# Two 3x3 convolutions that rotate through three pairs of PSUM banks for four, the two parts of a pair three taps apart for four

## The reference

```python
x = x + _L0_conv_ref(_gn(x), w_real, w_imag, b_real, b_imag)  # FFT, complex 3x3 convolution, inverse FFT
x = x + _L1_conv_ref(_gn(x))                                  # rows gated by the sign of a dot product
x = x + _L2_conv_ref(_gn(x), L2_conv_W)                       # 3x3 convolution, 16 to 16 channels
x = x + _L3_conv_ref(_gn(x), L3_conv_weight)                  # 3x3 convolution, 16 to 16 channels
```

## Time and profile before

| | us |
|---|---|
| median of 3 runs | 5523.62 (5523.53 to 5527.76) |
| the profiled execution, its own time | 5522.16 |
| its span, first to last instruction | 5520.4 |
| PE busy | 4636.8 (84%) |
| DVE busy | 3411.5 (62%) |
| ACT busy | 2593.9 (47%) |
| mean granted TensorE clock | 0.926 |

### The profile page before, as it was taken

How to read it: one execution, slowest core, us unless ns; L and a number is a source line. 1 busy time by engine, 2 the same in 40 slices (tenths; PEclk the granted TensorE clock), 3 DMA queues, 4 the chain that set the end, 5 groups by cost and what they waited for, 6 DMA issues and landing times. The chain is left out here.

```text
span 5520.4 us, 227169 instructions
## 1 busy us (share of the span) xinstructions
PE 4636.8 (84%) x84352; PEld 2919.4 (53%) x84352; DVE 3411.5 (62%) x10276; ACT 2593.9 (47%) x7377; POOL 956.5 (17%) x718
## 2 busy tenths in 40 slices
PE   3798699968999598995989959899599986988678
PEld 0455455545656365563655636566365644555455
DVE  0587816877178761887528874387835878168770
ACT  4355345553455434553445534456345553444434
POOL 0123101240022300223002230022201231012400
PEclk9999899988999799997999979999799998999889
DMA  5343024420344104441144401443024430232104
GB/s 167 101 123 95 3 86 133 122 75 3 114 125 125 52 11 126 124 125 33 34 122 123 126 15 45 133 125 114 2 62 140 123 92 3 88 96 68 37 3 125
DMA packets 294829, 471.65 MB, mean 85 GB/s; under 512 B 22288, under 2 KB 97104, under 8 KB 294224
## 3 DMA queue, kind: packets, MB, share of 16 engines
q1 hardware_dynamic: 294224, 462.41, 27.9%
HBM read 328.10 MB, written 134.22 MB: 84 GB/s over the span
## 5 line engine op out<-in xcount | busy, mean ns | idle before, releaser
L1123 PE MATMUL ps<-x,conv_s 32*32 32x512 f32 x49104 | 1816.1, 603 | 41.3 <-ACT shared L565 20.7
L1123 PEld LDWEIGHTS ps<-x,conv_s 32*32 32x32 f32 x49104 | 1253.6, 104 | 576.0 <-issue 338.5
L432 POOL TENSOR_TENSOR acc<-acc,x 128x512 f32<-128x512 f32 x512 | 669.0, 1307 | 4222.4 <-ACT x L494 4222.4
L1050 PE MATMUL ps<-hil,shared 128*128 128x256 f32 x4096 | 993.6, 386 | 0.0
L494 ACT ACTIVATE x<-ps,vec 128x256 f32 (+1 forms) x1024 | 490.1, 495 | 1002.8 <-PE ps L1050 1002.8
L1050 PEld LDWEIGHTS ps<-hil,shared 128*128 128x128 f32 x4096 | 740.4, 190 | 273.8 <-issue 194.1
L738 DVE SCALAR_TENSOR_TENSOR shared<-xin,trig 128x256 f32<-128x256 f32 x2048 | 811.7, 436 | 60.3
L565 ACT ACTIVATE shared<-ps,vec 64x512 f32<-64x512 f32 (+1 forms) x768 | 525.0, 684 | 574.4 <-PE ps L1123 564.8
L734 DVE TENSOR_SCALAR xin<-xin,vec 128x512 f32<-128x512 f32 x512 | 367.2, 717 | 626.9 <-DMA out<-shared 495.9
L1035 PE MATMUL ps<-shared 32*32 32x512 f32 x16384 | 669.3, 613 | 0.0
L554 ACT ACTIVATE x<-ps,vec 128x512 f32 x512 | 347.2, 684 | 471.5 <-PE ps L1123 471.5
(11 more groups left out here) (147 smaller groups left out, 3671.1 us busy)
## 6 DMA issues: line engine op xcount, KB each, us to landing
shared<-x SPq DMA_DIRECT2D x512, 256.0 KB
xin<-x SPq DMA_DIRECT2D x512, 256.0 KB
out<-shared SPq DMA_DIRECT2D x512, 256.0 KB
shared<-t_strip SPq DMA_DIRECT2D x576, 96.0 KB, 3.4
hil<-t_hil SPq DMA_DIRECT2D x1, 560.0 KB, 3.3
trig<-t_trig SPq DMA_DIRECT2D x1, 512.0 KB, 4.1
x<-t_bias SPq DMA_DIRECT2D x1, 512.0 KB, 5.1
x<-w_mix SPq DMA_DIRECT2D x1, 288.0 KB, 3.2
```

The lines of the kernel that those rows point to most:

```text
L432: nc.gpsimd.tensor_tensor(acc, acc, strip_of(s), ALU.add).then_inc(y_added, 1)
L1050: mm = pe.matmul(split_in(ps[:, BY + 2 * odd + e, :])[:, int(q < 2), :], xt[:, e, q, :], hil[:, q, 0:HALF], start=False, stop=True, skip_g ...
L1123: mm = pe.matmul(ps[TM * cg:TM * cg + TM, banks[k], :], conv_s[TM * rg:TM * rg + TM, kw, second, :], x1[TM * rg:TM * rg + TM, of, kw:kw + ...
```

## The change

`DEPTH` goes from 4 to 3 and `LAG` from `TAPS + 1` to `TAPS`. The places of the banks are now (0,1), (2,3), (4,5) in both convolutions; banks 6 and 7 are no longer used by pairs. The output slots of `evict3` keep their rotation of four pairs, under a name of its own. ACT's register loops are gone: all evictions of an image are written out. The wait for `v_bias3` on PE is gone.

```diff
-DEPTH = 4
-LAG = TAPS + 1
+DEPTH = 3
+SLOT_PAIRS = 4
+LAG = TAPS
@@ ACT
-                with act.Fori(0, PAIRS // DEPTH) as j:
-                    for e in range(DEPTH):
-                        evict2(j * DEPTH + e, banks2(e))
+                for n in range(PAIRS):
+                    evict2(n, banks2(n))
                 root(i, 4, ZV)
                 act.wait_ge(v_bias3, i + 1)
-                with act.Fori(0, PREPARING[0] // DEPTH) as j:
-                    for e in range(DEPTH):
-                        evict3(j * DEPTH + e, banks2(e), e, j)
-                for n in range(PREPARING[0], PREPARING[1] + 2):
-                    evict3(n, banks3(n), n % DEPTH, n // DEPTH)
+                for n in range(PAIRS):
+                    evict3(n, banks3(n), n % SLOT_PAIRS, n // SLOT_PAIRS)
                     if more and n == PREPARING[0] + 1:
                         root(i + 1, 0, 0)
                         root(i + 1, 1, ZV, ZR)
-                with act.Fori((PREPARING[1] + 2) // DEPTH, PAIRS // DEPTH) as j:
-                    for e in range(DEPTH):
-                        evict3(j * DEPTH + e, banks2(e), e, j)
@@ PE, first3
                     if kw == 0:
-                        if n == DEPTH - 1:
-                            pe.wait_ge(v_bias3, i + 1)
-                            due()
                         before = [k for k in range(n) if banks3(k) == banks3(n)]
```

## The result

| | before | after |
|---|---|---|
| median of 5 runs, us | 5524.2 (5523.53 to 5527.76) | 5553.69 (5545.6 to 5563.97) |
| profiled execution's own time | 5522.16 | 5553.69 |
| its span | 5520.4 | 5551.9 |
| mean granted TensorE clock | 0.926 | 0.926 |

The ratio is 1.0054, 95% interval 1.0039 to 1.0069: slower by 0.5%, 29 us, where +18 was forecast.

The account below looks back on a forecast made before the run. PE was taken to bound the convolutions. Terms -16.4 - 2.1 + 26.6 + 2 + 3 + 5 = +18.1 us on 5522.16 gave 5540.3; 5541.5 was predicted, own range 5534 to 5554, eight in ten 5524 to 5580.

Parts of the forecast that it names:

- What bounds, and the rates: Convolutions: bound by PE, 32.1 ns a record with both parts in a slot; a one-part slot costs nearly as much.
- The case with a drop after each of eight gaps: Pair 8: the clock falls after every new gap, 13.6 us for 2 in the sum, 5553 us; chance 0.07.
- The sign of being wrong, pairs over 3.1 us: Rolling loops: pairs taking longer than 3.1 us, with PE idle behind evictions or between parts, would refute the prediction.
- The wait at pair 8: conv3: pair 8 waits for pair 7's eviction, shifting all behind it by 3.32 us an image, +26.6 us.
- Rival 2: Pairs 8 to 13 don't follow pair 8's shift; faster, -18.5 us if none arrives, 5505 us; chance 0.12.
- The clock: PE's gap of some 2.3 us ahead of pair 8 may lower the granted clock: +2 us, bounds 0 to 13.6.
- The lag: Three rolling loops an image: one more full slot, two fewer single ones, -0.69 us each, -16.4 us in all.
- The thin waits: Less slack for evictions in rolling loops, +3 us, and for `halved` between a pair's two parts, +5 us.
- Rival 3: Thin margins cost 0.1 us at 464 pairs or 0.3 at 160 evictions, +46 to +48 us, 5588; chance 0.14.
- The forecast's loop: conv3's rolling loops, eviction to eviction: 9.05 us for three pairs against 9.24 today, so no longer.
- ACT written out: conv2's end: the last activation starts 0.26 us sooner once an image, -2.1 us; elsewhere only slack.
- All eight banks: The skill's rule implies a cost everywhere; the forecast expected bank shortage at pair 8 only, not in rolling loops.

Follow-up runs that it names:

- The wait alone: Kernel before, with only one wait more: pair 8 of conv3 waits for pair 7's eviction; ratio 1.0062.
- the swapped order: Places 2 and 1 for 1 and 2 in pairs 8 to 13: changed kernel 0.9947; kernel before 0.9965; four places, lag 3, ACT written out 0.9943.
- narrow stores: Only 64 of each strip's 512 output columns stored: kernel before 5451.1 us, lag 3 alone 5451.7, changed kernel 5476.3.
- filling: Changed kernel with 32 more records of matmuls per image ahead of pair 8's wait; ratio 1.0023.

## Why the prediction was right, and where not

**The number.** 5541.5 us were predicted and 5553.69 measured, inside the range and at the upper edge of the forecast's own (5534 to 5554). That it came so near is in part luck: in the ledger a term that was left out and one that was too small, +13.0 and +4.8 us, make up the difference, against 4 in the other direction. The case with a drop after each of eight gaps names 5553 us, but there were five drops, not eight, and the rest is the stalls.

**What bounds, and the rates.** Right: conv2's rate did not move, 32.1 ns a record. The sign of being wrong, pairs over 3.1 us, was badly set for conv3: the 3.08 us a pair came from conv2, and conv3's pairs 14 to 31 have a median spacing of 3.17 us in both kernels.

**The wait at pair 8.** Right in place, mechanism and size: 3.32 us forecast, 3.3 measured in the images without a drop (43.6 for 40.3), in all eight; the whole block shifted behind it. The wait alone and the swapped order show it from both sides. Rival 2 (the next stage doesn't follow) is out.

**The clock.** The mechanism was right, the term mis-sized: 2 us forecast, 6.8 measured at the two places, inside the bounds of 0 to 13.6. I took "most gaps leave no drop" from pair 14's eight gaps with one drop (two of the eight are in the earlier trace rows). The other profiles show that such a gap of 2.3 us is followed by a drop in none to seven of eight images, with the order around it hardly changed. One kernel's profile was no measure of the odds; the middle of the bounds would have been right here, and nothing found tells the odds ahead.

**The lag.** The structure gave what was summed, about: the remainder of the ledger, -14.6, lies between the forecast's -10.5 and -18.5. That is no proof of the lag's -16.4: with narrow stores the lag alone gave back 8 to 10 us, its drops taken off. What was left out of the sum is the stalls, +13 us in the profile. I had their row and charged them to ACT's code alone, as a bound of 10; written out alone that code makes 38.9 us of them for 36.1. The full stores make them. That the shorter lag makes them longer is only likely: the four kernels with full stores, lag 3 and no filling have 43 to 50 us, the four with lag 4 and four places 36 to 41, but lag 5 didn't lower them, and it is one profile each. Why the same stores hold PE longer there stays open. That what PE waits for is its instructions was argued, not shown: the profile says only that its weight loads wait for issue.

**The thin waits.** 8 us forecast; at most 4 in the ledger, 3 in the profiles with narrow stores. With three places and lag 4 conv3's pairs drew apart to 3.55 us, with lag 3 they don't. Rival 3, in which every pair pays, is out. The forecast's loop had the right sign but was 0.6 us short where it binds. PE's weight loads do wait longer for issue (446.8 us for 338.5), but not by the third place alone: with the lag alone it is 396.8, with pair 8's wait alone 389.5.

**ACT written out.** 0.26 us an image forecast, 0.32 found; too small for the runs. That the addresses are what takes the time fits another row: conv3's evictions, in register loops too before but at constant addresses, started 0.04 us after the last matmul there already (median).

**All eight banks.** The Trainium skill (Perfetto Trace Analysis, Matmul Optimizations) asks for the use of all eight PSUM banks. Here three places in the swapped order (0.9947) and four (0.9943) can't be told apart: what costs is not a bank left unused but a pair that takes the banks of the pair just completed. The fourth place is worth something with lag 4: three places cost 1.4% there, of which the wait at pair 8 alone is 0.6. The Trainium skill's other page cited (TensorE: Matmul & The Clock Gate, A second HAM failure mode: psum-queue depth-cycling) bears on it as forecast with little weight: idle gaps between groups did let the clock fall, in five images at 1.7 us. No bank's wait did so in the rolling loops; there the clock fell once, and twice before, behind stalls of 2 us. The forecast saw none of it before, since the earlier trace rows show conv2 alone; these are in conv3.

## What to carry to other kernels

When a rotation of buffers gets shorter, don't only check the steady loop: list for every point where the rotation is broken (a block with its own order) which buffer comes next and how long ago it was released. One reuse of a buffer just filled, eight times in 5.5 ms, cost more than the shorter lag's whole gain; permuting two places gave it back, and a wait that had stood at pair 14 all along. A gap of a few us on TensorE carries a risk of 1.7 us for the clock on top, and one profile doesn't tell how often it strikes.

## What the runs showed of the hardware

- After gaps of 2.3 us, alike in length and with nearly the same work on both sides, the granted clock fell from 2.4 to 1.2 GHz in 0 to 7 of 8 images, depending on the kernel; each fall lasted about 3.4 us and cost 1.7. Where matmuls cut the gap to 1.21 us, it stayed up in all eight.
- PE waits for no transfer in conv3, and still its stalls there, 36 to 50 us in eight images, hang on the stores: with an eighth of the bytes they were 0 to 0.6.
- ACT's activation started 0.04 us after the matmul's end where its addresses are constants, 0.36 us where they hang on a loop's register.
